# Idle-time products on TensorE, an earlier rest of the first gathered tile and an earlier Gelu table around the gate of a two-layer graph kernel

## What is computed

```python
# end of block 1: second convolution
agg = jax.ops.segment_sum(norm[:, None] * t[row], col, num_segments=n)
h = expmap0(agg)                                  # x = x + h
# block 2, on the layer-normed x: 8 experts, top 2, capacity 93
probs = jax.nn.softmax(xf @ gate_w.T + gate_b, axis=-1)
topw, topi = jax.lax.top_k(probs, TOPK)
wm = jnp.where(routed, w_te, -1.0)
sel_w, sel_idx = jax.lax.top_k(wm.T, cap)         # per expert: the 93 heaviest tokens
xg = xf[sel_idx]
h = jax.nn.gelu(jnp.einsum('ecd,edh->ech', xg, w1) + b1[:, None, :], approximate=False)
out = jnp.einsum('ech,ehd->ecd', h, w2) + b2[:, None, :]
of = jnp.zeros((T, D)).at[sel_idx.reshape(-1)].add((out * sel_w[..., None]).reshape(-1, D))
```

## Time and profile before

| | us |
|---|---|
| median of 3 runs | 2210.9 (2210.38 to 2211.02) |
| profiled execution, its own time | 2215.61 |
| span of the profiled execution | 2213.6 |
| TensorE busy in the span | 2117.3 (96%) |
| VectorE busy | 1509.2 (68%) |
| ScalarE busy | 1126.6 (51%) |
| GpSimd busy | 854.7 (39%) |
| granted TensorE clock, mean | 0.969 |

### The profile page before, as it was taken

The page is one execution under the profiler, slowest core; times in us unless marked ns, Lnnn a source line. Parts: engine busy times, 40 slices in busy tenths (PEclk is TensorE's granted clock), DMA queues, the critical chain, the costliest instruction groups (busy, mean ns, idle before and its releaser), DMA issues.

```text
span 2213.6 us, 36119 instructions
## 1 busy us (share of the span) xinstructions
PE 2117.3 (96%) x13358; PEld 1975.7 (89%) x13358; DVE 1509.2 (68%) x3183; ACT 1126.6 (51%) x3010; POOL 854.7 (39%) x688
## 2 busy tenths in 40 slices
PE   8876799999879999999999999999999999999998
PEld 7765566668769999999999999999999999999997
DVE  8736688855436667777667767667777767777766
ACT  4534466542444455555455555455555545555554
POOL 0000000000045455555445555545555545555551
PEclk9886899999979999999999999999999999999999
DMA  6000588871022111122111121211122211112110
GB/s 209 1 19 4 175 279 288 272 270 51 10 79 80 62 62 62 66 99 73 69 61 62 61 97 67 81 62 62 61 73 92 81 62 62 62 62 100 62 44 24
DMA packets 85687, 197.42 MB, mean 89 GB/s; under 512 B 5937, under 2 KB 10321, under 8 KB 85511
## 3 DMA queue, kind: packets, MB, share of 16 engines
q1 hardware_dynamic: 85512, 195.12, 25.4%
HBM read 193.75 MB, written 1.35 MB: 88 GB/s over the span
## 4 chain that ended last, share of the span: by engine, by line
PE 89%; ACT 5%; DVE 4%; issue 1%; POOL 0%; DMA 0%; SPq 0%; DVEq 0%; POOLq 0%; ACTq 0%
PE PS L54 80%; PE PS L53 5%; PE PS L57 4%; ACT HW L88 1%; ACT GT L88 1%; ACT HS L88 0%; DMA X<-in_x 0%; DVE OHs L68 0%; POOL SM L60 0%; ACT EE L88 0%; DVE SM L107 0%; DVE OHd L69 0%; DVE M L75 0%; DVE JU L66 0%; DVE X L60 0%
## 5 line engine op out<-in xcount | busy, mean ns | idle before, releaser
L54 PE MATMUL PS<-ZH,WS 128*128 128x314 f32 x4096 | 946.8, 312 | 0.0
L54 PEld LDWEIGHTS PS<-ZH,WS 128*128 128x128 f32 x4096 | 691.9, 189 | 0.0
L54 PE MATMUL PS<-ZL,WS 128*128 128x314 f32 x2048 | 625.7, 305 | 0.0
L60 DVE TENSOR_TENSOR ACC<-ACC,PS 128x314 f32<-128x314 f32 x1008 | 476.8, 477 | 197.0 <-PE PS L54 187.1
L54 PEld LDWEIGHTS PS<-ZL,WS 128*128 128x128 f32 x2048 | 387.7, 189 | 0.0
L60 POOL TENSOR_TENSOR WS<-RAW,WS 128x512 fp32r<-128x512 f32 x256 | 327.0, 1298 | 109.7 <-ACT WS L88 109.6
L60 POOL TENSOR_TENSOR ML<-MF,MH 128x400 fp32r<-128x400 f32 x128 | 134.0, 1047 | 412.3 <-ACT MH L88 412.1
L60 POOL TENSOR_TENSOR ZS<-ZS,ZQ 128x628 f32<-128x628 f32 x128 | 198.3, 1549 | 235.3 <-ACT ZQ L88 235.3
L88 ACT ACTIVATE ZH<-PS,g1T 128x628 fp32r<-128x628 f32 x128 | 100.4, 785 | 321.7 <-PE PS L54 321.7
L88 ACT ACTIVATE EE<-EE,SM 125x100 f32<-125x100 f32 x640 | 233.3, 375 | 13.8 <-DVE SM L68 11.0
L88 ACT ACTIVATE MF<-PS 128x400 f32<-128x400 f32 x128 | 64.6, 505 | 319.7 <-PE PS L53 319.7
(11 more groups left out here) (332 smaller groups left out, 3733.2 us busy)
## 6 DMA issues: line engine op xcount, KB each, us to landing
RAW<-in_L_ffn_wz_w SPq DMA_DIRECT2D x66, 1024.0 KB, 5.9
RAW<-in_L_ffn_w SPq DMA_DIRECT2D x64, 1024.0 KB, 7.3
RAW<-in_L_ffn_Wq_w SPq DMA_DIRECT2D x32, 1024.0 KB, 5.3
CB<-c_rows SPq DMA_DIRECT2D x32, 195.3 KB
RAW<-in_L_gnn_W SPq DMA_DIRECT2D x4, 1024.0 KB, 8.6
RAW<-in_L_ffn_Wkv_w SPq DMA_DIRECT2D x4, 1024.0 KB, 5.2
RAW<-in_L_ffn_Wk_T SPq DMA_DIRECT2D x2, 1024.0 KB, 6.0
WB<-w_rows SPq DMA_DIRECT2D x6, 305.2 KB
```

The costliest lines, as they stand in the source:

```text
L54: return self.q.matmul(o, l, r, start=start, stop=stop)
L60: return Nothing() if self.q is None else self.q.tensor_tensor(out=o, in0=a, in1=b, op=op)
```

## The change

`pe_busy` is a new helper of TensorE: n products of 128 rows by 94 columns with 512 moving columns into a PSUM bank that nobody reads. It is called at three places: 17 products on `W2H` after the squared norm of the second convolution is clipped, 13 products on `HW[0]` ahead of the gate's transposes, and 14 on `HW[0]` after the first tile of the first ranking. On VectorE `gathered_T(0)` goes ahead of the second ranking. On ScalarE a Gelu of one column goes behind the first ranking row, which loads Gelu's table there; what it writes nobody reads.

```diff
+        def pe_busy(q, bank, tile, n):
+            for _ in range(n):
+                q.mm(PS[0:94, bank, :], tile[:, 0:94], tile[:, 0:512], True, True)
...
                     i.then_inc(*ss_mm.up())
+            q.wait_ge(*row_v.of(1, "n2c"))
+            pe_busy(q, 6, W2H[:, 0, :], 17)
             for t in range(T5):
                 q.wait_ge(*row_v.of(1, ("m", t)))
...
+        c1g = SM[0:P, 440:441]
...
             rank_row(0)
+            q.act(c1g, ones[0:P, 0:1], ACT.Gelu).then_inc(*gate_a.up("gelu"))
             q.wait_ge(*gate_pe.of("wm"))
...
             row_tail(1)
+            gathered_T(0)
             rank_tiles(1, range(T5))
             rank_end(1)
-            gathered_T(0)
             for e in range(NE):
...
+            q.wait_ge(*w_hi.of(0, 1))
+            pe_busy(q, 6, HW[0], 13)
             turned(0)
...
             rank_row(0)
             weights_T()
+            q.wait_ge(*rank_v.of(0, 0, "eq"))
+            pe_busy(q, 2, HW[0], 14)
             dispatch(0)
```

## The result

The changed kernel takes 2200.64 us in the median of 5 runs (2197.61 to 2202.26), the kernel before 2210.9 in the median of 5 (2210.33 to 2214.79). The ratio is 0.9944 with a 95% interval of 0.9931 to 0.9957, 12.4 us of 2210.9; the two medians are 10.3 us apart. The forecast was 2198.4, and the time lies in its range. Its two halves were both off, in opposite directions: the clock gave more than was put down for it, XGL less.

The account below looks back on a forecast made before the run. TensorE, busy 96%, was taken as the bound, with time to win only where it waits or runs slowly. Terms 7.0 + 0 + 0.7 + 3.5 + 1.3 = 12.5 us, off the 2210.9 median: 2198.4, range 2192.5 to 2205.0.

Parts of the forecast that it names:

- the clock: The three groups of idle products keep TensorE at full clock: 0.7 us at the aggregation, 3.5 gate, 1.3 first dispatch.
- XGL: First expert: XGL ahead of the second ranking starts TensorE's first up 8.0 us earlier; 7.0 us remain after waiting for chunk 8.
- chunk 8 late: Rival: loads of chunks 8 and 9 contend with the small ones ahead, XGL's part is 4.0; 9.5 us gained, chance 0.15.
- The aggregation: 17 products ahead of the aggregation let it run at higher clock: 0.7 us, between -0.1 and 1.9.
- The gate: 13 products ahead of the gate's transposes keep the clock high for part of the gate: 3.5 us, between -0.8 and 5.7.
- The dispatch: 14 products in the first ranking let the first expert's dispatch start warm: 1.3 us, between 0 and 2.9.
- Gelu: Gelu's table load of 1.28 us on ScalarE moves earlier; worth 0, since ScalarE then waits for chunk 8 anyway.
- Chunk 8 in time: Rival: ScalarE is never stopped in the first expert, XGL with the table gives 11.0; 16.5 us gained, chance 0.12.
- The clock gains nothing: Rival: at each place the clock falls before the dense part, or products run slowly before the gate; 6.2 us gained, chance 0.09.
- slower: Rival: the products' SBUF reads and PSUM writes slow VectorE and ScalarE beside them, making the kernel slower; chance 0.02.
- XGL isn't what TensorE waits for: Rival: the first expert's first up waits for a later thing than XGL; 5.5 us gained, chance 0.02.
- transposes don't hold the clock: Rival: the gate's transposes count for nothing, its 13 products give 2.0, not 3.5; 10.7 us gained, chance 0.10.

## Why the prediction was right

**XGL.** Right in every link of the mechanism: the 8.0 us on TensorE, SP's order, ScalarE stopped at `weights(6)`, `HS` and the Gelus behind it, TensorE idle behind `down(0, 0)`. Counted from the first `up`, SP asked for chunk 8 at 9.1 us (the forecast's sum has 9.2), and from the copy of chunk 8 to `WSP` it is 6.24 us (6.26). The term was mis-sized, 7.0 against 3.7 in the first trace of the change and 5.0 to 5.6 in the seven others. The step that failed is "a load takes 5.4 us to land": that was the median of seven loads, three of which took 8.1 to 9.1, and chunk 8, right behind six others and with chunk 9 behind it, took 7.9 (6.9 to 7.9 in all). The cold stretch was too short as well: four slow products, 0.8 us, were allowed for, and the second dispatch and `down(0, 1)` are at 0.50 from 239 to 246, with 1.6 us lost behind `WSP` in that trace. The 2.5 us of the load and these 0.8 are the 3.3 that the term lacks. The rival "chunk 8 late" had the longer load, with 4.0 for XGL's part, at a chance of 0.15.

**The clock.** 5.5 was forecast and 8.9 came in the first trace (8.2 by the time of the products alone). The aggregation gave 1.9, the upper bound, in nine of ten traces; the lower case exists, as the products alone show. The gate gave 4.2 in the first trace and up to 5.4 in others, where 3.5 had been taken between "the clock falls some 3 us after the products" and "the transposes hold the clock". The clock lasted longer than 3 us in every one of the nine traces: 5.2 us in the first, and to the gate's end in five. Why it falls within the gate in the other four stays open. The dispatch gave 2.8 or nothing, and 1.3 lay between. Both branches of that step occur: in the first trace the 14 products ran slowly and reached the dispatch, in the second trace of the same kernel they ran fast and left a pause of 2.99 us.

**Gelu.** Zero beside XGL, as forecast and for the reason given; alone it is worth 1.4 us of the path.

**The sum.** Two errors of 3.3 and 3.4 us cancelled in the first trace; in the second trace of the same kernel, with 5.3 for XGL and 7.3 for the clock, two of 1.7 and 1.8 did. That the sum came so near was luck.

**The other rivals.** "Chunk 8 in time" needed an edit of its own. "The clock gains nothing", "slower" and "XGL isn't what TensorE waits for" are out by the stages above, and "transposes don't hold the clock" by the run with idle transposes and by the gate's 4.1 us or more, where that rival had 2.0.

## What to carry to other kernels

When a wait goes, walk every queue to the next thing that can be late, and price a load there by loads in the same crowd, not by a median over the stretch; then mend that queue in the same edit. Products that nobody reads pay where they end exactly where the real work starts, so place them by what that work waits for, and check both levels of the clock at which they can run. Two parts that shorten the same wait don't add up: measure each with the other taken away.

## What the runs showed of the hardware

With idle transposes in place of the products, transposes and products of 8 columns ran for 10 us at 2.4 GHz (180 to 190 us at 1.00). The gate's own transposes and small products, started at 1.2 GHz in the kernel before, ran 12 us without raising the clock. In the changed kernel the clock fell at 188.3 us while products of 8 columns ran (187.1 to 191.0), so these alone did not hold it there. A load of 1 MB took 4.9 to 5.4 us to land where no smaller load went just ahead of it, and 6.9 to 7.9 right behind six smaller ones and with the next chunk's load behind it. The same code in front of the change ended between 145.70 and 149.88 us from trace to trace. A difference of 4 us in a single pair of traces means nothing there, and its cause was not looked for.
